# Four graph-attention layers on one core: a new order of work in the stages between the heads

## The chip, the cores and the metric

The kernel runs on one NeuronCore of a Trainium2 chip. The metric is the time of one execution on the device in microseconds (us), the median of several runs. Five engines work side by side, each through its own instruction list in order: TensorE (PE in the rows), VectorE (DVE), ScalarE (ACT), GpSimd (POOL) and SyncE (SP, which here only issues transfers). They wait for each other through semaphores that are written out by hand.

## The reference

`x` is (8 graphs, 1024 nodes, 128 features) and `adj` one 1024 x 1024 matrix for all graphs. Four layers follow each other, each closed by a residual and a norm:

```python
x = _layernorm(x + _L0_gnn_ref(x, adj, ...))   # 4 heads; inside: layernorm(attention @ Wo + bo + x) * gamma + beta
x = _layernorm(x + _L1_gnn_ref(x, adj, ...))   # 4 heads; inside: attention @ wo + bo
x = _layernorm(x + _L2_gnn_ref(x, adj, ...))   # 1 head of 128; leaky-relu scores; inside: elu(attention)
x = _layernorm(x + _L3_gnn_ref(x, adj, ...))   # 4 heads of 32; leaky-relu scores; inside: elu(attention)
```

Layer 0 thus has two norms after its attention (an inner one with gamma and beta, an outer one), the others have one.

## The kernel before

The kernel alternates between `node(stage)`, stages 0 to 4, and `heads(layer)`, layers 0 to 3. `heads` holds the attention and is not touched. `node(s)` closes layer s-1 (residual, norm) and opens layer s: it makes queries, keys and values (or, in stages 2 and 3, rows and columns of scores) of the new x and stores them to device memory. Stage 0 has nothing to close, stage 4 nothing to open.

A stage is a loop of rounds `i` from `-SKEW[stage]` to 7, written out in full on every engine. In round i each engine does the *closing* work of graph `f = i + SKEW[stage]` and the *opening* work of graph `i`. Before, SKEW is 2 in stage 1 and 1 in stages 2 to 4. So stage 1 has ten rounds, stages 2 to 4 nine, and in a round without a graph f (or a graph i) that half is left out.

Closing graph f, stages 1 and 2: PE transposes the attention's result (`turn_context`, L911) into PSUM banks 0 and 1; ACT copies it (`context`, L740); PE multiplies it (`contract`, L946, counted as y_ps) into banks 2 and 3; DVE adds x (`add_x`, L1262, event y) and takes mean and variance (`statistics`, L1249, event var); POOL raises them to the power -1/2 (`power`, event rstd); ACT applies that, eight instructions for the eight blocks of a graph (`norm`, L723; event xn). In stage 1 the first such norm is `inner_norm` (event z), then DVE does `scaled` (times gamma, plus `xplus`, which POOL made of x and beta in `plus_beta`, event xb), a second `statistics`, and ACT does `outer_norm`. In stages 3 and 4 the attention's result needs the ELU instead of a multiplication: ACT makes exp and relu of it (`below_zero`, L747, into the buffer `neg`), and DVE adds.

Opening graph i: PE transposes xn (`turn_x`, L917) into banks 4 and 5; ACT copies it (`turned`); PE multiplies queries and keys (`queries_keys`) or score rows (`rows_of`), then values into banks 0 and 1 (`by_blocks(0, ...)`), in stages 2 and 3 also columns (`columns_of`). ACT copies the first two (`high_parts`), then rounds the values to bf16 (`first_part`); DVE takes what is left (`project`: cv L1298, and the low parts of queries and keys), ACT rounds that (`second_part`), POOL what remains then (`last_part`, L650). SP stores all of it.

Since context and values share banks 0 and 1, `turn_context` waits until ACT and DVE have read the values (`values_read`).

The order inside a round of stage 1 before:

```
ACT:  context(f) turned(i) high_parts(i) first_part(i) inner_norm(f) second_part(i) outer_norm(i+1)
DVE:  add_x(f) statistics(f) project(i) scaled(i+1) statistics(i+1)
POOL: plus_beta(f) power0(f) last_part(i) power(i+1)
PE:   turn_context(f) turn_x(i) contract(f) queries_keys(i) values(i)
SP:   store_x(i) load(f+2) store_parts(i)
```

The loads of graph f+2 use the buffers of graph f, so SP waits for y, cT_ps and (stage 1) xb of f first (`used`).

## Time and profile before

| what | us |
|---|---|
| median of 3 runs (3216.36 to 3223.19) | 3221.73 |
| time of the profiled execution | 3225.56 |
| its span in the trace | 3223.8 |
| granted TensorE clock, mean | 0.83 of full speed |
| stage 1, first load issued to last copy of values by ACT | 749.3 to 1003.9 |
| stage 2, the same | 1755.9 to 1915.6 |
| stage 3, the same | 2258.6 to 2398.3 |
| stage 4, first load to last norm | 3109.1 to 3220.1 |

The table is read as a map: all that the diff touches lies in these four stretches (and in stage 0, up to about 125 us). The profiled execution has 1.8 us outside its span. A busy share over the whole span says little about a stage; what ends the waits in one round of each stage says more. A row of the windows view holds, from the left: the stretch, its length, the busy us (and instructions) of PE, PEld, DVE, ACT and POOL, the granted PE clock (1.00 is 2.4 GHz, 0.50 is 1.2 GHz), the busy share of the DMA engines and GB/s.

### The profile page before, as it was taken

The numbers are of one execution on the slowest core, as the hardware profiler recorded it, in microseconds if no ns is written. First come the engines' busy times: TensorE is split into PE (matmuls) and PEld (weight loads), VectorE is DVE, ScalarE is ACT, GpSimd is POOL, SyncE is SP. The second block draws the span as 40 slices with busy tenths as digits, with TensorE's granted clock in tenths as the row PEclk, the third lists the DMA queues.
The fourth block names the chain that finished last, engine by engine and source line by source line (L and its number), as shares of the span: only waits on it lengthen the run. The fifth ranks groups of instructions, "written<-read, shape, count | busy, mean of one in ns | idle before, by whom it ended". The sixth has DMA issues, their size and how long they took to land.

```text
span 3223.8 us, 90525 instructions
## 1 busy us (share of the span) xinstructions
PE 2378.1 (74%) x32777; PEld 1657.8 (51%) x33112; DVE 2195.8 (68%) x4654; ACT 1588.1 (49%) x2273; POOL 1827.9 (57%) x1837
## 2 busy tenths in 40 slices
PE   5588888884434988888886766888457999999950
PEld 3366666664332555555554544667234666666630
DVE  4499999994443777777776335452558988888943
ACT  3354444452441444444443543444555777777763
POOL 2388888885330665555566333444225777777851
PEclk9788888886665999999998667999667988888975
DMA  7822322223433112121212641110541111111134
GB/s 249 273 71 76 83 73 71 71 57 71 159 137 120 53 48 55 44 55 44 55 45 72 162 157 58 53 31 15 164 122 38 48 47 48 47 39 48 48 65 98
DMA packets 299864, 263.65 MB, mean 82 GB/s; under 512 B 193080, under 2 KB 257080, under 8 KB 299504
## 3 DMA queue, kind: packets, MB, share of 16 engines
q1 hardware_dynamic: 294896, 241.82, 27.3%
q0 software_dynamic: 4608, 16.78, 1.4%
q8 instruction: 257, 4.21, 0.5%
q14 instruction: 103, 0.84, 0.1%
HBM read 162.84 MB, written 95.36 MB: 80 GB/s over the span
## 4 chain that ended last, share of the span: by engine, by line
PE 29%; issue 15%; DVE 14%; ACT 4%; POOL 2%; DMA 2%; SPq 1%; DVEq 1%; POOLq 0%; ACTq 0%
PE ps L1107 11%; PE ps L1066 5%; DVE full L1393 4%; DVE full L1383 2%; PE ps L1004 2%; ACT xn L723 2%; POOL xc L333 2%; PE ps L1018 2%; PE ps L966 1%; PE ps L1064 1%; PE ps L1059 1%; DVE xn L1480 1%; DVE rden L1477 1%; PE ps L928 1%; PE ps L1051 1%
## 5 line engine op out<-in xcount | busy, mean ns | idle before, releaser
L333 POOL TENSOR_TENSOR xc<-part 128x512 f16<-128x512 f32 x1536 | 1579.2, 1054 | 805.1 <-ACT part L858 650.5
L1107 PE MATMUL ps<-vs,part 128*128 128x33 bf16 (+1 forms) x13824 | 847.6, 188 | 46.6 <-DVEq L1484 44.5
L1107 PEld LDWEIGHTS ps<-vs,part 128*128 128x128 bf16 x13824 | 676.2, 101 | 357.8 <-issue 198.0
L1107 PE MATMUL ps<-vs,xc 128*128 128x33 bf16 (+1 forms) x9216 | 777.0, 186 | 5.6 <-issue 5.6
L1107 PEld LDWEIGHTS ps<-vs,xc 128*128 128x128 f16 x9216 | 594.8, 99 | 0.0
L858 ACT ACTIVATE part<-ps 128x512 f32<-128x512 f32 x512 | 305.8, 597 | 432.6 <-PE ps L1051 432.4
L1393 DVE CUSTOM_DVE_ANT_0 full<-ps,mask_n 128x512 bf16<-128x512 f32 x512 | 353.0, 690 | 161.8 <-DVE top L1393 64.0
L1383 DVE CUSTOM_DVE_ANT_0 full<-ps,mask_n 128x1024 bf16<-128x1024 f32 x320 | 390.3, 1220 | 99.2 <-PE ps L1004 70.7
L840 ACT ACTIVATE part<-cv,lift 128x1024 f32<-128x1024 f32 x256 | 294.7, 1151 | 324.7 <-DVE cv L1414 298.1
L1066 PE MATMUL ps<-qs,sel 128*128 128x512 f32 x640 | 418.1, 655 | 14.3 <-ACT ps L832 14.2
L1047 PE MATMUL ps<-qs,ks 128*128 128x512 f32 x512 | 289.3, 568 | 120.8 <-DVE cv L1414 93.4
L1426 DVE SCALAR_TENSOR_TENSOR cv<-ks,colx,ps 128x512 f32<-128x512 f32 x320 | 238.7, 746 | 174.6 <-PE ps L1066 135.1
L858 ACT ACTIVATE part<-cv,cols 128x512 f32<-128x512 f32 x320 | 229.8, 718 | 239.0 <-DVE cv L1426 229.1
L1414 DVE SCALAR_TENSOR_TENSOR cv<-ps,mask_t 128x1024 f32<-128x1024 f32 x256 | 311.8, 1219 | 46.8 <-PE ps L1047 23.9
L1018 PE MATMUL ps<-ks,qs 96*128 96x512 f32 x512 | 253.1, 505 | 117.2 <-DVE top L1393 94.9
L1051 PE MATMUL ps<-qs,ks 97*128 97x512 f32 x512 | 307.7, 601 | 0.5
L858 ACT ACTIVATE part<-ps,colx 128x512 f32<-128x512 f32 x320 | 215.1, 672 | 74.2 <-PE ps L1066 69.2
L1089 PE MATMUL ps<-vs,part 128*128 128x99 bf16 x2048 | 233.0, 213 | 1.8 <-POOL xc L333 1.8
L1089 PEld LDWEIGHTS ps<-vs,part 128*128 128x128 bf16 x2048 | 164.5, 99 | 129.6 <-issue 106.3
L832 ACT ACTIVATE ps<-ks,colx 128x512 f32<-128x512 f32 x316 | 218.7, 692 | 11.5
L1091 PE MATMUL ps<-vs,xc 128*128 128x66 bf16 x2048 | 219.5, 195 | 0.0
L928 PE MATMUL ps<-ident,xn 128*128 128x128 f32 x256 | 56.5, 393 | 204.9 <-ACT xn L723 200.9
(151 smaller groups left out, 3591.8 us busy)
## 6 DMA issues: line engine op xcount, KB each, us to landing
qs<-q_d SPq DMA_DIRECT2D x224, 128.0 KB
ks<-k_d SPq DMA_DIRECT2D x224, 128.0 KB
ks<-row_d SPq DMA_DIRECT2D x40, 512.0 KB
vs<-v_d SPq DMA_DIRECT2D x96, 198.0 KB
q_d<-part SPq DMA_DIRECT2D x32, 512.0 KB
k_d<-part SPq DMA_DIRECT2D x32, 512.0 KB
ctx_d<-xn SPq DMA_DIRECT2D x96, 128.0 KB, 1.7
xc<-ctx_d SPq DMA_DIRECT2D x96, 128.0 KB, 4.3
```

The lines of the kernel that those rows point to most:

```text
L333: eng.tensor_tensor(plo[:, r, :], prob[:, r, :], phi[:, r, :], ALU.subtract).then_inc(low_done(layer, u, s)[0], 1)
L840: act.activation(prob[:, r:r + 2, :], arg[:, a:a + 2, :], ACT.Exp, scale=2.0 * CLIP, bias=lift[:, 0:1]).then_inc(s_exp, 2)
L858: act.activation(prob[:, r, :], src, ACT.Exp, **more).then_inc(s_exp, 1)
L1018: pe.matmul(bank, qs[0:96, n, it * P:(it + 1) * P], ks[0:96, n, cut], start=True, stop=True).then_inc(s_nsc, 1)
L1047: mm = pe.matmul(bank, ks[:, n, blk_j], qs[:, n, cut], start=True, stop=True)
L1051: mm = pe.matmul(bank, ks[0:97, n, blk_j], qs[0:97, n, cut], start=False, stop=True)
L1066: mm = pe.matmul(bank, sel[:, 2, :], qs[:, n, cut], start=False, stop=True, skip_group_check=True)
L1089: pe.matmul(ps[:, 6 + c, at_a:at_a + V3], phi[:, r, it * P:(it + 1) * P], vs[:, n, at_v:at_v + V3], start=opens, stop=False, skip_group_ch ...
L1107: mm = pe.matmul(acc, half[:, r, it * P:(it + 1) * P], vs[:, n, at:at + width], start=opens and h == 0 and v == 0, stop=h == 1 and v == 1, ...
L1383: dve.tensor_tensor_reduce(junk[:, :], pf[:, 4 * HALF:6 * HALF], mask_n[:, k, :], 1.0, LOWEST, ALU.add, ALU.max, accum_out=top[:, k, 0:1]) ...
L1393: dve.tensor_tensor_reduce(junk[:, 0:HALF], ps[:, 4 + c, :], mask_n[:, it, c * HALF:(c + 1) * HALF], 1.0, LOWEST, ALU.add, ALU.max, accum_ ...
L1414: dve.scalar_tensor_tensor(arg[:, a:a + 2, :], ps[:, r:r + 2, :], -0.5, mask_t[:, j:j + 2, c * HALF:(c + 1) * HALF], ALU.max, ALU.min).the ...
```

## The change

Eight edits, all in `node`:

1. SKEW of stages 2 and 3 goes from 1 to 2, so that these stages have ten rounds and graph i's xn is made two rounds before it is transposed.
2. `contract` writes y into banks 0 and 1, over the transposed context; `turn_context` of the next graph now waits for y of the graph before (DVE's `add_x`), not for the values.
3. The values get banks 2 and 3 for themselves (in stage 0 the keys move to banks 0 and 1).
4. In stage 1 DVE begins the round with `scaled(i+1)` and its statistics, and does `add_x(f)` and `project(i)` after them.
5. In stage 1 ACT does `outer_norm(i+1)` after `first_part(i)`, then `second_part(i)`, and `inner_norm(f)` last.
6. In stage 1 POOL begins with `power(i+1)`; `plus_beta(f)` goes to the end of its round.
7. In stage 1 SP loads graph f+2 after it has stored the parts of graph i.
8. In stages 3 and 4 `below_zero` runs one graph ahead: `below_zero(f+1)` stands in front of `outer_norm(f)`, `neg` has two buffers, and the wait for y is one graph looser.

```diff
-SKEW = (0, 2, 1, 1, 1)
+SKEW = (0, 2, 2, 2, 1)
...
-        xT, neg = cv[:, 2, :], cv[:, 3, :].rearrange("p (t f) -> p t f", f=F)
+        xT = cv[:, 2, :]
+        neg = [cv[:, k, :].rearrange("p (t f) -> p t f", f=F) for k in (0, 3)]
...
-            at = (6, 4)[w] if stage else (6, 2)[w]
+            at = (6, 4)[w] if stage else (6, 0)[w]
...
                     if stage and i >= 0:
                         store_x(i)
-                    if f + 2 < GRAPHS:
+                    if stage != 1 and f + 2 < GRAPHS:
                         used(f)
                         load_graph(stage, f + 2)
                     if stage < 4 and i >= 0:
                         store_parts(i)
+                    if stage == 1 and f + 2 < GRAPHS:
+                        used(f)
+                        load_graph(stage, f + 2)
...
+                    if stage == 1 and 0 <= i + 1 < GRAPHS:
+                        power(stage, "", i + 1)
                     if stage == 1 and f < GRAPHS:
-                        plus_beta(f)
                         power(stage, "0", f)
                     if stage > 1 and f < GRAPHS:
                         power(stage, "", f)
                     if stage < 4 and i >= 0:
                         last_part(i)
-                    if stage == 1 and 0 <= i + 1 < GRAPHS:
-                        power(stage, "", i + 1)
+                    if stage == 1 and f < GRAPHS:
+                        plus_beta(f)
...
-                    act.wait_ge(s_ev["y"], before("y", stage, b))
-                    act.activation(neg[:, :, :], cs[:, b % 2, :, :], ACT.Exp).then_inc(s_ev["ex"], 1)
+                    act.wait_ge(s_ev["y"], before("y", stage, b) - 1)
+                    act.activation(neg[b % 2], cs[:, b % 2, :, :], ACT.Exp).then_inc(s_ev["ex"], 1)
...
-                    if stage > 2 and f < GRAPHS:
-                        below_zero(f)
+                    if stage > 2 and f == 0:
+                        below_zero(0)
                     if stage < 4 and i >= 0:
                         turned(i)
                         high_parts(i)
                         first_part(i)
+                    if stage > 2 and f + 1 < GRAPHS:
+                        below_zero(f + 1)
+                    if stage == 1 and 0 <= i + 1 < GRAPHS:
+                        outer_norm(i + 1)
+                    if stage < 4 and i >= 0:
+                        second_part(i)
                     if stage == 1 and f < GRAPHS:
                         inner_norm(f)
-                    if stage < 4 and i >= 0:
-                        second_part(i)
-                    if stage == 1 and 0 <= i + 1 < GRAPHS:
-                        outer_norm(i + 1)
...
                 def turn_context(b):
                     pe.wait_ge(s_load[b % 2], load_at(stage, b // 2))
-                    values_read(max(a, 0))
+                    pe.wait_ge(s_ev["y"], before("y", stage, b))
...
-                    pe.wait_ge(s_ev["y"], before("y", stage, b))
-                    by_blocks(2, cT, wts[:, 4 * (stage - 1) + 3, :], 2 * stage - 1, "y_ps")
+                    by_blocks(0, cT, wts[:, 4 * (stage - 1) + 3, :], 2 * stage - 1, "y_ps")
...
-                        by_blocks(0, xT, wts[:, 4 * stage + 2 if stage < 2 else 6 + stage, :],
+                        by_blocks(2, xT, wts[:, 4 * stage + 2 if stage < 2 else 6 + stage, :],
...
+                    if stage == 1 and 0 <= i + 1 < GRAPHS:
+                        scaled(i + 1)
+                        statistics(i + 1, 1, "")
                     if stage and f < GRAPHS:
                         add_x(f)
                         statistics(f, 0 if stage == 1 else 1, "0" if stage == 1 else "")
                     if stage < 4 and i >= 0:
                         project(i)
-                    if stage == 1 and 0 <= i + 1 < GRAPHS:
-                        scaled(i + 1)
-                        statistics(i + 1, 1, "")
```

## Rows read from the trace of the kernel before

**Rows 1.** The page, part 1: busy time and share of the span.
```profile
PE 2378.1 (74%) x32777; PEld 1657.8 (51%) x33112; DVE 2195.8 (68%) x4654; ACT 1588.1 (49%) x2273; POOL 1827.9 (57%) x1837
```

**Rows 2.** Windows: one round of stages 1, 2, 3 and 4, in this order.
```profile
852.17:880.41 28.24, 12.08 (x60) 9.33 (x60) 13.51 (x38) 12.42 (x23) 9.67 (x10) 0.68 0.49 159
1803.08:1820.29 17.21, 13.44 (x70) 11.01 (x70) 7.14 (x22) 9.80 (x17) 8.10 (x12) 0.70 0.70 201
2294.80:2310.85 16.05, 9.70 (x44) 6.07 (x44) 10.09 (x26) 10.94 (x17) 4.44 (x5) 0.71 0.61 166
3142.13:3155.11 12.98, 0.00 (x0) 0.00 (x0) 4.74 (x18) 5.27 (x11) 2.35 (x4) 0.50 0.53 121
```

**Rows 3.** Timeline of ACT, stage 1: start, duration, line, out<-in, idle before and releaser.
```profile
760.35 1.02 ACT L743 ACTIVATE cv<-ps 128x1024 f32<-128x1024 f32 x1 [20.66 <-PE ps L914]
...
859.49 1.11 ACT L767 ACTIVATE part<-ps,bcol 128x1024 fp32r<-128x1024 f32 x1 [4.14 <-PE ps L957]
...
863.37 1.05 ACT L782 ACTIVATE vbuf<-ps 128x1024 bf16<-128x1024 f32 x1 [1.11 <-PE ps L941]
...
877.32 3.18 ACT L723 ACTIVATE xn<-full,rstd 128x128 f32<-128x128 f32 x8 [8.87 <-POOL rstd L634]
...
989.76 3.18 ACT L723 ACTIVATE xn<-full,rstd 128x128 f32<-128x128 f32 x8 [9.57 <-POOL rstd L634]
...
1003.94 1.05 ACT L782 ACTIVATE vs<-ps 128x1024 bf16<-128x1024 f32 x1 [1.11 <-PE ps L941]
```

**Rows 4.** Timeline of DVE, stage 1.
```profile
766.01 1.22 DVE L1268 TENSOR_TENSOR full<-ps,xc 128x1024 f32<-128x1024 f32 x1 [14.53 <-PE ps L941]
...
781.05 1.23 DVE L1268 TENSOR_TENSOR full<-ps,xc 128x1024 f32<-128x1024 f32 x1 [11.46 <-PE ps L941]
...
857.81 1.23 DVE L1268 TENSOR_TENSOR full<-ps,xc 128x1024 f32<-128x1024 f32 x1 [11.44 <-PE ps L941]
...
869.28 2.97 DVE L1279 TENSOR_TENSOR full<-full,vs 128x1024 f32<-128x1024 f32 x1
872.29 1.64 DVE L1252 BATCH_NORM_STATS2 bns<-full 128x6 f32<-128x128 f32 x8
873.97 0.64 DVE L1257 BATCH_NORM_AGGREGATE mv<-bns 128x2 f32<-128x6 f32 x8
```

**Rows 5.** Timeline of ACT, stage 2.
```profile
1811.16 1.01 ACT L773 ACTIVATE part<-ps 2x1024 f32<-2x1024 f32 x1 [4.91 <-PE ps L966]
...
1915.63 1.03 ACT L782 ACTIVATE vs<-ps 128x1024 bf16<-128x1024 f32 x1
```

**Rows 6.** Timeline of DVE, stage 2.
```profile
1792.19 1.23 DVE L1268 TENSOR_TENSOR full<-ps,xc 128x1024 f32<-128x1024 f32 x1 [12.25 <-PE ps L941]
...
1809.40 1.22 DVE L1268 TENSOR_TENSOR full<-ps,xc 128x1024 f32<-128x1024 f32 x1 [7.99 <-PE ps L941]
```

**Rows 7.** Timeline of ACT, stage 3.
```profile
2278.74 1.02 ACT L759 ACTIVATE cv<-ps 128x1024 f32<-128x1024 f32 x1
...
2299.55 1.01 ACT L773 ACTIVATE part<-ps 8x1024 f32<-8x1024 f32 x1 [3.73 <-PE ps L966]
...
2304.65 1.08 ACT L787 ACTIVATE vs<-cv 128x1024 bf16<-128x1024 f32 x1 [1.35 <-DVE cv L1298]
...
2398.28 1.02 ACT L782 ACTIVATE vs<-ps 128x1024 bf16<-128x1024 f32 x1
```

**Rows 8.** Timeline of ACT, stage 4.
```profile
3126.04 3.18 ACT L723 ACTIVATE xn<-full,rstd 128x128 f32<-128x128 f32 x8 [7.85 <-POOL rstd L634]
...
3142.13 1.04 ACT L749 ACTIVATE cv<-xc 128x1024 f32<-128x1024 f32 x1
...
3216.95 3.18 ACT L723 ACTIVATE xn<-full,rstd 128x128 f32<-128x128 f32 x8 [7.68 <-POOL rstd L634]
```

**Rows 9.** Timeline of SP's queue, stage 4: the four context loads of one graph.
```profile
3134.37 3.69 SPq L416 DMA_DIRECT2D xc<-ctx_d  x4
```

**Rows 10.** DMA issues of stage 4: count, KB each, median us to landing.
```profile
xc<-ctx_d SPq DMA_DIRECT2D x32, 128.0 KB, 4.2
```

## What the change will do, and by how much

> **What bounds the kernel now.** I began with the page's busy shares [rows 1]: no engine is above 74% of the span, so waits set the pace somewhere. All that the diff touches lies in the stages between the heads, so I laid a window over one round of each stage [rows 2]. There no engine is near full: of a round of 28.24 us in stage 1 ACT works 12.42, DVE 13.51, PE 12.08; in stage 2 (17.21 us) PE 13.44 and ACT 9.80; in stage 3 (16.05 us) ACT 10.94; in stage 4 (12.98 us) ACT 5.27 and nobody more. A round is a loop of waits. The timelines give the loop, and the reader is to look at the brackets. In stage 1 ACT waits 8.87 us for POOL's rstd before the outer norm [rows 3]: DVE first takes apart the values of graph i, and only then scales graph i+1. The next round's context copy stands behind that norm, and y behind the copy. In stage 2 the two waits are those for PE, 4.91 us among them [rows 5]. In stage 3 ACT waits 3.73 us for the rows and 1.35 us for DVE, the rest is its own work: 10.94 + 3.73 + 1.35 = 16.0, the round [rows 2, 7]. In stage 4 ACT waits 7.68 us for rstd of the graph whose ELU it has just made [rows 8].
>
> **Stage 1.** What is removed is the wait of the outer norm for DVE's second half. I lay out a new round on ACT, from the start of context(f) at 0.
> - Context to y: at 760.35 ACT starts the copy with nothing else on PE, at 766.01 DVE starts on y: 5.66 us [rows 3, 4]. That is at the lower clock.
> - y to the queries' copy: 859.49 - 857.81 = 1.68. To the values' copy: 863.37 - 859.49 = 3.88 [rows 3, 4]. So values at 11.2.
> - Values 0.95; then outer_norm(i+1), 3.1 (a row's 3.18 less the overlap with the next); second_part 1.0; inner_norm(f) 3.1. Next context at 19.4. The same by counting: 12.42 of work and some 7 of waits for PE that remain.
>
> Is each input there? scaled(i+1) needs z from the end of the round before: DVE starts at 0.1 and takes 1.25 + 1.25 + 2.32 for scaling, addition and statistics [rows 4]. The addition at L1279 took 2.97 where it met POOL's last_part, against 1.23 for such a size alone [rows 4]; now scaling meets plus_beta instead. I allow 1.7 more: var(i+1) at 6.6. From the end of the aggregation at 874.61 to the norm at 877.32 are 2.71 [rows 3, 4]: rstd at 9.3, needed at 12.2. y at 5.66 waits up to 1 us for DVE, then var0(f) by 10.2 and rstd0 by 12.9, needed at 16.3. The values' remainder on DVE ends at 12.2 + 3.6 = 15.9 (1.23 for vf and the two low parts), when PE may turn the next x, as the next round needs at 19.4. All of it is covered; if the cover of rstd (2.9 us) were gone, each us would lengthen the round by one.
>
> The moved load: plus_beta(f) is now last on POOL, after last_part, which follows second_part at 16.3; POOL's whole work is 9.67 us a round [rows 2], so these two end by about 21.5. Only then does SP issue load(f+2), behind four stores of queries and keys, one of values, one x. Issue takes 4.1 (0.4 + 3.69), the last context load lands 4.2 after its issue [rows 9, 10]; in all some 9 us with the stores in front, at 30.5, or 11 into the next round. turn_context(f+2) comes up on PE after that round's values, at 11.2, and turn_x behind it is held until 15.9 anyway; 4 us are to spare.
>
> Clock: PE's work of a round now lies in shorter stretches with shorter pauses. The y term above is priced at the lower level; I add 0.5 for queries that still begin low. Round: 19.9.
>
> Ends: y(1) stays at 781.05. statistics 3.58, rstd 2.71, inner norm 3.1: round 0 starts at 790.4. Six rounds of 19.9: 909.8. Round 6 has no context: the values' copy comes 11.0 after the end of the outer norm before it (989.76 + 3.18 to 1003.94 [rows 3]), of which 2.1 are transposes already made: 8.9; outer_norm(7) then ends at 909.8 + 8.9 + 0.95 + 3.2 = 922.9; 0.6 until DVE frees the keys' bank; 11.0: last values at 934.5. Before 1003.94. **Gain 69.4.** Bounds: the ACT sum with no clock term (19.4) 72, a round of 22.5 53.
>
> **Stage 2.** One round more, xn(i) early, banks apart. From the context copy 0: y at 5.66 instead of 6.32 (1803.08 [rows 2] to 1809.40 [rows 6]), since PE no longer turns x first; the rest of the round, 10.89, stays: 16.55. PE then works 13.4 of 16.5 and may find the higher clock a bit earlier: 16.4. Ends: y(1), without turn_x before it but behind outer_norm(0), is 0.9 earlier, 1791.3; 3.6 + 2.7 + 3.1 to the start of round 0, 1800.6; six rounds, 98.4, to 1899.0; round 6 without a graph f takes 13.1 (values' copy 7.5 after that of x, DVE up to the columns 3.5, turning 2.1); then 7.5: 1919.6. Before 1915.63 [rows 5]. **Loss 4.0**: the freed wait is worth less than the added round. Bounds: y at 3.5 after the copy, with PE at the higher clock (the 4.58 us from the start of `contract` to y halved to about 2.4), makes the round 14.4 and a gain of 8; rows too at the lower clock (18.1), a loss of 14.
>
> **Stage 3.** The ELU of f+1 stands where ACT waited 1.35 for DVE, so that wait is covered; the 3.73 for the rows stay, as x is now turned early but the copy and the product still follow each other: 14.7. Round 0's x copy moves behind outer_norm(1): from 2278.74 to 2282.4. Then 7 x 14.7 + 7.5: 2392.8, before 2398.28 [rows 7]. **Gain 5.5.** Bounds: 0 (SP's store of x now has to be done within the same round, it is issued some 10 us ahead of the norm) and 17 (rows at the higher clock, 13.0).
>
> **Stage 4.** The loop ELU, add, statistics, power, norm is opened. ACT works 5.27 [rows 2]; power(f) must wait for xn(f-1), since rstd has one buffer, so norm to norm is at least 2.7 + 3.1 = 5.9. But the loads follow: SP issues load(f+2) only behind the store of xn(f-1). From xn(f-1): store 0.4, x 0.4, three context issues 2.8, 4.2 to landing [rows 9, 10], and about 1.2 because the stored 512 KB now lie directly in front: 9.0. Then ELU 2.15 and norm 3.2 give xn(f+1): 14.4 for two graphs, 7.4 a graph with the gaps between instructions. The DMA engines agree: 0.53 x 12.98 = 6.9 us of work per graph [rows 2]. Norms from 3126.04: two distances of 5.9 and five of 7.4, last one at 3174.8 instead of 3216.95 [rows 8]. **Gain 42.** Bounds: 45 if the store costs nothing in front; 27 with 9.5 us a graph.
> The Trainium skill ("DMA: Bandwidth & Descriptors", section "Why small descriptors are slow") counts a fixed overhead of about 3 bus cycles per packet, which for the 128-byte pieces of the context loads leaves 4 of 7. By its 435 GB/s a graph's 512 KB would take an estimated 2.1 us. The window's 6.9 us leave about 4.4 for them after two large transfers of 1.25, so the trace shows them slower than the page has it; by the page the sum would be some 5 us lower.
>
> **Stage 0** keeps its waits, the banks only change names: 0. The heads: 0.
>
> **Sum.** 69.4 - 4.0 + 5.5 + 42.1 = 113. The profiled execution of 3225.56 (span 3223.8) would become 3112.6; the median of the runs is 3.8 lower, so 3221.7 - 113 = 3109.
>
> **Rivals.**
> 1. *PE holds the higher clock in the closer rounds.* For it: the pauses shrink, in stage 2 to 3 us of 16. Against: in stage 2 PE is busy 13.44 of 17.21 even now and has 0.70 [rows 2]. Stage 1 rounds of 17.3 (16 more), stage 2 a gain of 8 instead of a loss of 4, stage 3 a gain of 17: 3109 - 16 - 12 - 12 = 3069.
> The Trainium skill ("TensorE: Matmul & The Clock Gate", section "HAM oscillation — how this bites in real kernels") says that pauses make the clock fall and each burst begin cold, and that work without long pauses keeps it up. It speaks for this rival; row 0.70 at 78% busy speaks for less.
> 2. *The loads bind.* DMA work is 0.49 x 28.24 = 13.8 us a round in stage 1, 12.0 in stage 2 [rows 2]; if the bursts collide, stage 1 goes to 24 and stage 4 to 9.5: 25 + 15 less gain, 3149.
> 3. *DVE and POOL collide more than allowed*, as POOL's two additions are now adjacent and DVE starts just there: rstd late by 3 us a round in stage 1, 22.9, 18 less gain: 3127.
> 4. *Slower.* The load of stage 1, put behind xb and the stores, misses its graph and PE waits for it in order. It has 4 us to spare; to eat 113 us over six rounds it must be 4 + 19 = 23 us late. At 25 late: 6 x 2 over the even point, 3234.
> 5. *The change doesn't do what it says in stage 1*: DVE still finds z or xb late, the round stays at 28.2; 3178. The z norm ends the ACT round, which speaks against it.
>
> **Chances.** As worked out 0.54 (its own range 3092 to 3127); rival 1 0.12, rival 2 0.15, rival 3 0.11, rival 4 0.04, rival 5 0.04. What is left out of 3076 to 3150 is rivals 1, 4 and 5, 0.20. 0.2% (6 us) is about what a measurement of this kernel tells from no change. Faster 0.94, same 0.02 and slower 0.04.
>
> **What the profile after would show.** Right: y-to-y distances of 20, 16.4, 14.7 us in stages 1 to 3; the outer norm of stage 1 with no wait for POOL; ten rounds in stages 2 and 3; norm-to-norm 5.9 once and then 7.4 in stage 4, with ACT's exp waiting for the DMA. Wrong: an rstd wait of some us in stage 1 (rival 3), `turn_context` waiting for a DMA there (2, 4), PE clock above 0.8 in the stages (1).

## The result and the profile after

The changed kernel takes 3119.5 us (median; 3117.63 to 3143.97) against 3220.43 of before: 0.9701 of its time, 95% interval 0.9658 to 0.9744. Run again, beside experiments 1 to 3, it took 3123.56, ratio 0.9702 (0.9673 to 0.9731); one of the 17 executions of the kernel before that were timed with these, 4280.64 us at a granted clock of 1.00, is not counted. Predicted were 3109, in a range of 3076 to 3150. The execution whose trace is read here is a long one, 3143.97 (span 3142.2); the third row below shows why, a stretch in which the change alters nothing.

Windows of the profile after, from SP's first load for a stage to the first load of the heads behind it: stage 1, stage 2, heads 2, stage 3, stage 4. The columns are those of [rows 2]: length, busy time of PE, its weight loads, DVE, ACT, POOL, granted clock, DMA share, GB/s.
```profile
750.60:947.38 196.78, 112.72 (x480) 82.61 (x480) 104.33 (x305) 98.24 (x176) 75.17 (x82) 0.70 0.59 183
1688.71:1864.93 176.22, 109.30 (x560) 83.54 (x560) 57.12 (x176) 78.17 (x120) 64.76 (x90) 0.66 0.55 157
1864.93:2217.65 352.72, 278.76 (x2850) 213.65 (x2850) 151.49 (x328) 133.87 (x192) 135.81 (x145) 0.81 0.14 44
2217.65:2366.25 148.60, 82.28 (x368) 50.36 (x368) 85.28 (x209) 87.43 (x128) 40.69 (x42) 0.67 0.52 143
3065.16:3142.20 77.04, 0.00 (x0) 0.00 (x0) 37.89 (x144) 42.78 (x80) 22.37 (x32) 0.50 0.73 164
```
The same stretches cut from the kernel before, and from the changed kernel run again:

| us | before | after | after, again | predicted change |
|---|---|---|---|---|
| up to the first heads | 129.8 | 133.7 | 133.1 | 0 |
| heads 0 | 619.5 | 616.9 | 615.0 | 0 |
| stage 1 | 267.1 | 196.8 | 196.5 | -69.4 |
| heads 1 | 739.5 | 741.3 | 742.6 | 0 |
| stage 2 | 169.9 | 176.2 | 178.4 | +4.0 |
| heads 2 | 332.8 | 352.7 | 332.8 | 0 |
| stage 3 | 152.7 | 148.6 | 148.4 | -5.5 |
| heads 3 | 697.7 | 698.9 | 698.7 | 0 |
| stage 4 | 114.8 | 77.0 | 76.7 | -42.1 |

Heads 2 has the same instructions in all three (2850 weight loads). In the twelve other profiles of this study, the kernel before among them, it takes 331.5 to 334.7 us at a granted clock of 0.85 or 0.86; this one shows 352.7 at 0.81. The second profile has the normal value, and there the sum is -101.6 of the predicted -113.

What the reader can see of the single steps. Stage 1, ACT's timeline, profile after:
```profile
857.98 1.11 ACT L772 ACTIVATE part<-ps,bcol 128x1024 fp32r<-128x1024 f32 x1 [6.41 <-PE ps L963]
...
861.86 1.05 ACT L787 ACTIVATE vs<-ps 128x1024 bf16<-128x1024 f32 x1 [1.11 <-PE ps L948]
862.80 3.16 ACT L728 ACTIVATE xn<-full,rstd 128x128 f32<-128x128 f32 x8
865.87 1.07 ACT L792 ACTIVATE vs<-cv 128x1024 bf16<-128x1024 f32 x1
866.84 3.17 ACT L728 ACTIVATE full<-full,rstd 128x128 f32<-128x128 f32 x8
869.91 1.00 ACT L748 ACTIVATE cv<-ps 128x1024 f32<-128x1024 f32 x1
...
934.99 1.05 ACT L787 ACTIVATE vs<-ps 128x1024 bf16<-128x1024 f32 x1 [1.11 <-PE ps L948]
```
The outer norm at 862.80 has no bracket where it had 8.87 us of wait for POOL [rows 3]. From the values' copy (861.86) to the next context copy (869.91) ACT works without a gap. What remains are its waits for PE. The distance between the starts of `add_x` of two graphs, y to y, is the length of a round: 18.7 to 20.2 us in the full rounds. The last values come at 934.99; 934.5 was forecast.

Stage 2, PE's timeline, the same profile:
```profile
1776.93 1.07 PE L921 MATMUL ps<-ident,xc 128*128 128x128 f32 x8
1779.90 1.94 PE L935 MATMUL ps<-ident,xn 128*128 128x128 f32 x8 [1.90 <-DVE colp L1325]
1783.68 0.61 PE L940 MATMUL ps<-bias,ones_b 65*128 65x512 bf16 x1 [1.84 <-ACT cv L748]
1784.08 1.92 PE L948 MATMUL ps<-wts,cv 128*128 128x128 f32 x8
...
1788.06 2.27 PE L972 MATMUL ps<-cv,aa 128*2 128x512 f32 x4
```
There are two pauses of under 2 us a round. From the first of them on PE runs at the 1.2 GHz level: eight transposes take 1.94 us where those in front of the pause took 1.07. The clock comes back within the rows' product (L972), so that 10.2 us of this round are at the low level and the rest at 2.4 GHz (granted clock 0.70). Stage 2's round is 16.5 to 17.0 us instead of the forecast 16.4.

Stage 4, ACT's timeline, the same profile:
```profile
3083.97 3.19 ACT L728 ACTIVATE xn<-full,rstd 128x128 f32<-128x128 f32 x8 [4.91 <-POOL rstd L638]
...
3096.05 1.06 ACT L754 ACTIVATE cv<-xc 128x1024 f32<-128x1024 f32 x1 [2.14 <-DMA xc<-ctx_d]
...
3102.83 1.06 ACT L754 ACTIVATE cv<-xc 128x1024 f32<-128x1024 f32 x1 [1.46 <-DMA xc<-ctx_d]
...
3106.52 3.18 ACT L728 ACTIVATE xn<-full,rstd 128x128 f32<-128x128 f32 x8 [1.46 <-POOL rstd L638]
...
3118.81 1.06 ACT L754 ACTIVATE cv<-xc 128x1024 f32<-128x1024 f32 x1 [2.89 <-DMA xc<-ctx_d]
...
3135.29 3.18 ACT L728 ACTIVATE xn<-full,rstd 128x128 f32<-128x128 f32 x8 [3.04 <-POOL rstd L638]
```
The wait of 7.68 us for rstd [rows 8] is down to 1.46 or nothing between the first norm and the last, and the exps wait for their context loads, as forecast. Seven norm-to-norm distances add to 3135.29 - 3083.97 = 51.3 us, 7.3 each; the sum had 48.8.

### The profile page after: what moved, and what is told of

Read it like the earlier page. It is cut to its first block, busy times and chain, and to the rows that moved or that the text cites. A ratio compares the mean times of both kernels' runs of the same rounds, so it can differ in the third digit from the quotient of the medians.

```text
span 3142.2 us, 90847 instructions
## 1 busy us (share of the span) xinstructions
PE 2413.1 (77%) x33112; PEld 1668.6 (53%) x33112; DVE 2194.8 (70%) x4654; ACT 1585.7 (50%) x2273; POOL 1829.2 (58%) x1837
## 4 chain that ended last, share of the span: by engine, by line
PE 38%; issue 22%; DVE 22%; ACT 7%; POOL 3%; DMA 2%; DVEq 1%; SPq 1%; ACTq 0%; POOLq 0%
PE ps L1113 13%; PE ps L1072 4%; DVE xn L1458 4%; DVE full L1399 4%; PE ps L1010 3%; DVE full L1389 2%; PE ps L948 2%; PE ps L1053 2%; ACT xn L728 2%; PE ps L1065 2%; DVE cv L1420 2%; PE ps L1070 2%; POOL xc L334 2%; PE ps L1024 2%; PE ps L972 2%
## 5 line engine op out<-in xcount | busy, mean ns | idle before, releaser
L1095 PEld LDWEIGHTS ps<-vs,part 128*128 128x128 bf16 x2048 | 164.2, 99 | 129.8 <-issue 103.9
L1056 PE MATMUL ps<-mask_t,ident_b 128*128 128x512 bf16 x512 | 205.0, 400 | 0.4
```

Of the source, the lines that this page charges most:

```text
L1095: pe.matmul(ps[:, 6 + c, at_a:at_a + V3], phi[:, r, it * P:(it + 1) * P], vs[:, n, at_v:at_v + V3], start=opens, stop=False, skip_group_ch ...
```

## The experiments

Lengths of stages are cut from the traces as above. The changed kernel's are 196.5, 178.4, 148.4 and 76.7 us (after, again); stages that an edit doesn't touch came out within 2.5 us of that. An edit's effect on a stage is read from one profile each, so a difference of 2 to 3 us says nothing. The rest scatters more: the time up to the first heads lay anywhere from 129.3 to 133.7, heads 0 from 613.8 to 619.5, and heads 3 from 693.7 to 712.5.

**1. The kernel again, and the skew of stage 2 back at 1.**

> The changed kernel unchanged, profiled and timed again. In its first profile (3142.2 us) the attention of layer 2, which the diff does not touch, took 352.7 us from its first unit load to the next stage's first load, against 332.8 before, at a granted clock of 0.83 against 0.90; three other executions of the same kernel were 22 to 26 us shorter. Theory: TensorE falls into one of two rhythms there, by chance of phase, and in a profile near 3117 us this stretch is back near 333 us with a clock near 0.90, while the stages between the heads keep their lengths of 196.8, 176.2, 148.6 and 77.0 us within 2 us. Rival: the change itself lengthens it (other bank use, other landing times); then it is 352 us again and the 25 us are lost elsewhere. Ratio to before 0.968.

The theory held: 3123.56 us, heads 2 back at 332.8 us, the stages 196.5, 178.4, 148.4 and 76.7. (The expectation's clocks, 0.83 and 0.90, leave out the two ends of heads 2; over the whole of it they are 0.81 and 0.86.) What made it slow once is open. Two of the executions of the kernel before timed here also lie over 20 us above its median (3241.46 and 3243.39, clock 0.828 against 0.835), without a trace that shows where.

> The changed kernel with SKEW of stage 2 back at 1, all else kept. My theory (the freed wait is worth less than the added round): stage 2 goes from 176.2 us back to about 170 (round near 17.2 us, nine rounds), so this kernel is 6 us faster than the changed one. Rival (the skew pays, the 6 us come from the shared banks): the length stays at 176 or grows to 190, because y and the context now share banks 0 and 1 and turn_context waits for y.


```diff
-SKEW = (0, 2, 2, 2, 1)
+SKEW = (0, 2, 1, 2, 1)
```
3115.04 us, ratio 0.9677 (0.9644 to 0.9710); stage 2 takes 168.9 us, with y-to-y distances of 17.0 to 17.1 against 16.5 to 17.0. So the second graph ahead shortens hardly any round in stage 2, and the round more costs 7.3 or 9.5 us, by the first or the second profile of the changed kernel. The clock is part of that: the stage's granted clock is 0.71 here and 0.66 or 0.65 there. With fillers on PE (experiments 6 and 9) the same two skews give 165.9 and 152.5 us, 13.4 apart. The 169.9 of before the change lie within the scatter of 168.9, so the separate banks by themselves do nothing here that can be told.

**2. The ELUs in turn.**

> The changed kernel with the ELU of a graph made in its own round again (two buffers and the looser wait kept). My theory: stage 4 goes from 77 us back to 115 (round 13.0 us), stage 3 from 148.6 to 158 (its round from 14.5 to 15.8, since the 1.35 us wait for DVE is open again); together 45 us slower than the changed kernel, ratio to before 0.983. Rival: the two buffers and the looser wait alone already give part of it, stage 4 at 90 to 100 us.


```diff
-                    if stage > 2 and f == 0:
-                        below_zero(0)
+                    if stage > 2 and f < GRAPHS:
+                        below_zero(f)
...
-                    if stage > 2 and f + 1 < GRAPHS:
-                        below_zero(f + 1)
```
3172.93 us, ratio 0.9846 (0.9811 to 0.9882). Stage 3 161.8, stage 4 115.3 us. ACT in its stage 4:
```profile
3098.45 3.18 ACT L728 ACTIVATE xn<-full,rstd 128x128 f32<-128x128 f32 x8 [7.67 <-POOL rstd L638]
3101.54 1.04 ACT L754 ACTIVATE cv<-xc 128x1024 f32<-128x1024 f32 x1
```
The loop of before is back with its wait of 7.67 and its round of 12.98 [rows 2, 8]; the buffers and the looser wait alone give nothing. The early ELU is worth all of stage 4's gain, and 13.4 us in stage 3: with the skew of 2 but ELUs in turn that stage is 9 us longer than before the change.

**3. DVE's and POOL's old order in stage 1**, all else changed.

> The changed kernel with DVE's and POOL's old place for the second norm of stage 1 (after the values' remainder), ACT's new order kept. My theory: this one edit carries stage 1. The outer norm waits again for DVE: values 12.2, remainder 3.6, scaling and statistics 4.8, power 2.7, norm 3.1, second part 1.0, inner norm 3.1: a round of 30 us, slower than before the change (28.2); stage 1 about 265 us instead of 196.8, ratio to before near 0.99. Rival: the freed banks and the later inner norm carry it; then the round stays at 20 to 23 us.


```diff
                 for i in range(-SKEW[stage], GRAPHS):
                     f = i + SKEW[stage]
-                    if stage == 1 and 0 <= i + 1 < GRAPHS:
-                        scaled(i + 1)
-                        statistics(i + 1, 1, "")
                     if stage and f < GRAPHS:
                         add_x(f)
...
                         project(i)
+                    if stage == 1 and 0 <= i + 1 < GRAPHS:
+                        scaled(i + 1)
+                        statistics(i + 1, 1, "")
```
(and POOL's `power` of i+1 behind that of f.) 3204.47 us, ratio 0.9949 (0.9922 to 0.9977). Stage 1 takes 281.1 us in rounds of 30.7, 14 more than before the change; the theory had 265 and rounds of 30. ACT's timeline there:
```profile
872.96 1.05 ACT L787 ACTIVATE vbuf<-ps 128x1024 bf16<-128x1024 f32 x1 [1.11 <-PE ps L948]
885.16 3.18 ACT L728 ACTIVATE xn<-full,rstd 128x128 f32<-128x128 f32 x8 [11.15 <-POOL rstd L638]
```
The wait is back at 11.15, more than the 8.87 of before. By the orders, that is because ACT now has the late norm ahead of two operations that were ready, 4.0 us of work.

**4. ACT's old order in stage 1**, with DVE's and POOL's new one.

> The changed kernel with ScalarE's order of before in stage 1 (first norm, second part of V, second norm), and DVE's and POOL's new order. Theory A, formed on the run in which DVE and POOL alone had their old order (round 30.7 us, longer than the 28.2 of before): the two orders belong together, since a round of the new kernel is set by xn, TensorE and the evictions of q, k and V, after which ScalarE starts the second norm without a wait for POOL. With the old order the first norm (3.17) and the second part (about 1) come in between, so xn is ready some 4 us later: round about 23.5 instead of 19.7, stage 1 about 197 + 7 x 3.8 = 224 us, the whole about 3150. Theory B: only DVE's order mattered, ScalarE's could have stayed: round 19.7 to 20.5, stage 1 up to 203, the whole at 3122 to 3130.


```diff
-                    if stage == 1 and 0 <= i + 1 < GRAPHS:
-                        outer_norm(i + 1)
-                    if stage < 4 and i >= 0:
-                        second_part(i)
                     if stage == 1 and f < GRAPHS:
                         inner_norm(f)
+                    if stage < 4 and i >= 0:
+                        second_part(i)
+                    if stage == 1 and 0 <= i + 1 < GRAPHS:
+                        outer_norm(i + 1)
```
One run, 3128.2 us; stage 1 201.4 us, y-to-y 18.3 to 20.1. Theory A fell, B holds: DVE's order is what counts. The full rounds are 19.7 us on average, as in the changed kernel; most of the 5 us lies in one distance at the start of the stage (18.3 against 14.5). ACT's timeline of it:
```profile
863.97 3.18 ACT L728 ACTIVATE full<-full,rstd 128x128 f32<-128x128 f32 x8 [0.38 <-POOL rstd L638]
867.06 1.06 ACT L792 ACTIVATE vs<-cv 128x1024 bf16<-128x1024 f32 x1
868.03 3.17 ACT L728 ACTIVATE xn<-full,rstd 128x128 f32<-128x128 f32 x8
871.10 1.00 ACT L748 ACTIVATE cv<-ps 128x1024 f32<-128x1024 f32 x1
```
Both norms still stand between the values' copy and the context copy, only swapped, so the next round begins at the same place; my theory had counted xn's delay and forgotten that the context copy, not xn, heads the round.

**5. The skew of stage 3 back at 1**, ELUs still ahead.

> The changed kernel with a skew of 1 instead of 2 in stage 3, as before the change; the ELUs are still begun a graph ahead and V keeps its own banks. Theory A (the second graph ahead is what takes POOL's rstd and the norm off the chain that sets stage 3's round): round 15.5 to 16, as in the kernel before (16.05), less one round at the start: stage 3 148.4 + 8 x 1.3 - 9 = about 150, the whole within 3 us of the changed kernel. Theory B (the skew carries the gain in full): round 16.7, stage 3 about 158, the whole +10. Theory C (the ELU begun ahead and V's banks alone do it, as stage 2 showed for its skew): round 14.5, stage 3 about 140, the whole -8.


```diff
-SKEW = (0, 2, 2, 2, 1)
+SKEW = (0, 2, 2, 1, 1)
```
3128.31 us, ratio 0.9714 (0.9674 to 0.9755); stage 3 160.2 us, rounds of 16.7 to 17.0. Its timeline of PE:
```profile
2282.38 1.97 PE L935 MATMUL ps<-ident,xn 128*128 128x128 f32 x8 [5.60 <-ACT xn L728]
2285.46 3.58 PE L972 MATMUL ps<-cv,aa 128*8 128x512 f32 x4 [1.11 <-ACT cv L764]
```
PE waits for a norm that stands behind the ELU on ACT. Theory B: in stage 3 either half of the change alone makes it longer (160.2 and 161.8 against 152.7 before); the two together make 148.4. Both halves have the banks apart; no run shows what the banks do in this stage by themselves.

**6. PE's pauses in stage 2 filled.**

> The changed kernel with 16 further matmuls of the bias row (65x512, results not used) in each full round of stage 2: 8 between the turned context and the turned x, 8 between the turned x and the context's contraction, where TensorE pauses for 1.90 and 1.84 us. Theory A: these two pauses are what keeps the granted clock at the low level in the half of the round behind them (turned x 1.94 us, contraction 1.92 a half, rows 2.36, where the other half shows 1.07, 1.05); filled, the clock stays high, each filler of 8 takes about 1.8 us and so fits its pause, and a round goes from 17.0 to about 14 us (TensorE's work at high clock 9 to 10 us, with the waits for ScalarE behind it): stage 2 178.4 - 6 x 3 = about 160, the whole about 3105. Theory B: the clock stays low in that half, the fillers take about 3.4 us each in place of a pause of 1.9, and each round is 1.5 to 3 us longer: stage 2 187 to 196, the whole about 3135.


```diff
+                def filler(bank):
+                    for _ in range(8):
+                        with_bias(bank, 0)
...
+                    if has_f and has_a and stage == 2:
+                        filler(5)
                     if has_a:
                         turn_x(i)
+                    if has_f and has_a and stage == 2:
+                        filler(2)
```
3116.19 us, ratio 0.9674 (0.9634 to 0.9714). Stage 2 falls to 165.9 us, rounds of 14.47; theory A had 160 and the whole at 3105. Most of the gain is lost again in heads 3, which takes 707.3 us in this profile instead of 698.7, for a reason that is open. PE's timeline:
```profile
1784.38 1.07 PE L921 MATMUL ps<-ident,xc 128*128 128x128 f32 x8
1785.29 1.89 PE L940 MATMUL ps<-bias,ones_b 65*128 65x512 bf16 x8
1787.35 1.06 PE L935 MATMUL ps<-ident,xn 128*128 128x128 f32 x8 [0.17 <-DVE colp L1333]
1788.25 1.89 PE L940 MATMUL ps<-bias,ones_b 65*128 65x512 bf16 x8
1791.13 0.39 PE L940 MATMUL ps<-bias,ones_b 65*128 65x512 bf16 x1 [0.99 <-ACT cv L748]
1791.36 1.05 PE L948 MATMUL ps<-wts,cv 128*128 128x128 f32 x8
```
x8 in 1.05 where it was 1.92: the 2.4 GHz level holds through the whole round, and each filler fits its pause. The work left to do is the same, so the 12.5 us (10 to 14 against the 176.0 to 179.5 of all profiles that have this stage unchanged) are the price of the clock in this stage. The Trainium skill ("TensorE: Matmul & The Clock Gate", section "A second HAM failure mode: psum-queue depth-cycling") tells of a kernel in which small idles between groups of matmuls, not long waits, made the clock go up and down; the trace agrees, with pauses of 1.90 and 1.84 us.

**7. Stage 4: the loads ahead of the store.**

> The changed kernel, but in stage 4 SP issues the loads of graph f+2 before the store of graph i, so that they wait for y (which frees the buffers) and no longer for xn. In the changed kernel y's second operation ends 0.5 us before xn in one round and 2.1 us before it in another, and the store's issue takes 0.4 us. Theory A (the loads' start sets ScalarE's wait for them): loads start 0.9 to 2.4 us earlier a round, a round of 7.2 falls to 6.0 to 6.5, stage 4 from 76.7 to 69 to 72 us. Theory B (what sets it is the issue of the four context loads, 4.8 us, and the transfers behind them, with the 16 DMA engines 74% busy over the stage): the loads land hardly earlier and stage 4 stays at 75 to 77 us. The whole moves by 7 us at most.


```diff
-                    if stage and i >= 0:
+                    if stage and stage < 4 and i >= 0:
                         store_x(i)
...
                         load_graph(stage, f + 2)
+                    if stage == 4 and i >= 0:
+                        store_x(i)
```
3116.7 us, ratio 0.9687 (0.9635 to 0.9738), not to be told from the changed kernel as a whole; stage 4 72.9 us, between the theories and nearer to A, rounds of 6.76, one of 7.14. ACT's timeline:
```profile
3072.13 1.04 ACT L756 ACTIVATE cv<-xc 128x1024 f32<-128x1024 f32 x1
3073.21 1.15 ACT L758 ACTIVATE cv<-cv,unit 128x1024 f32<-128x1024 f32 x1
3075.81 3.18 ACT L730 ACTIVATE xn<-full,rstd 128x128 f32<-128x128 f32 x8 [1.45 <-POOL rstd L640]
3078.90 1.04 ACT L756 ACTIVATE cv<-xc 128x1024 f32<-128x1024 f32 x1
```
No exp waits for a load any more, though the DMA engines are 79% busy over the stage.

**8. Stage 4: long pieces.**

> The changed kernel, with the four context loads of a graph in stage 4 each as 1 KB pieces into two whole rows of blocks, in place of 128-byte pieces scattered over all rows: the same bytes, but the context's columns then stand in another order than the reference's, so its output is another. It takes the cost of the short pieces away and leaves the order of all engines. Theory A (the short pieces set ScalarE's wait for the context loads, 1.1 to 3.0 us in most rounds of stage 4): the issue of the four loads falls from 4.8 to 1.5 to 2 us, the exps never wait for DMA, the round is then that of the norms (ScalarE 5.4 us busy, or 1.45 us of wait for POOL's rstd as well) at 5.5 to 6.7 us in place of 7.2, stage 4 is 64 to 71 us instead of 76.7. Theory B (bytes or the start of the loads set it): 74 to 77.


```diff
                     for k in range(4):
+                        if stage == 4:
+                            sp.dma_start(cs[:, q, 2 * k:2 * k + 2, :],
+                                         one(ctx_d, b * 4 + k).rearrange("a p t f -> (a p) (t f)")
+                                         ).then_inc(s_load[q], 16)
+                            continue
```
This kernel leaves out the reference's order of the context's columns, as the expectation says. One run, 3113.6 us; stage 4 72.0 us, again between the theories. SP's timeline of it, and under it that of the changed kernel at the same point:
```profile
3067.07 0.39 SPq L430 DMA_DIRECT2D out<-xn  x1
3067.51 0.58 SPq L411 DMA_DIRECT2D xc<-x_d  x1
3068.13 2.59 SPq L418 DMA_DIRECT2D xc<-ctx_d  x4
```
```profile
3093.94 0.40 SPq L425 DMA_DIRECT2D out<-xn  x1
3094.38 0.58 SPq L411 DMA_DIRECT2D xc<-x_d  x1
3095.00 5.08 SPq L417 DMA_DIRECT2D xc<-ctx_d  x4
```
With the same bytes the issue of the four loads takes 2.59 us instead of 5.08 and the DMA share falls from 0.73 to 0.55. But an earlier start (7) gives the same stage to within 1 us: beyond 4 to 5 us neither helps. A loop over two graphs is then left. In the trace of experiment 7 it is norm 3.1, ELU 2.2, y to the end of the aggregation 5.0 and power 3.2, each with the gap behind it: 13.5 us, which is two rounds of 6.76.

**9. Fillers in stages 1 to 3**, with the skew of 1 in stage 2 from experiment 1 and the loads of experiment 7.

> Four edits to the changed kernel, each in a stage of its own, so that each is read from its stage's length. Stage 1: 16 filler matmuls of the bias row before the turned context, 12 behind the turned x (where TensorE pauses 4.1 and 2.8 us a round). Stage 2: a skew of 1, and 20 fillers before the turned x (the pause there is 4.8 us with a skew of 1, and 8 + 8 fillers held the clock at 2.4 GHz with a skew of 2). Stage 3: 16 fillers before the turned x, 5 behind it (pauses 3.7 to 4.1 and 1.2). Stage 4: the loads of graph f+2 ahead of the store. Theory A (the pauses hold the clock low in all three stages, and TensorE at the low level is on the chain that sets each round): stage 1: the contraction 3.9 to 2.0 us, round 19.7 to about 17.7, length 196.5 to about 181; stage 2: round 14.5 with one round fewer than with a skew of 2, 165.9 to about 155; stage 3: turned x 1.94 to 1.07 and rows 3.58 to 1.9, round 14.5 to 12.0, length 148.4 to about 128; stage 4 72.9 again. The whole about 3060. Theory B (only stage 2 was so near the bound that filling helped): stages 1 and 3 at their lengths or up to 3 us a round longer by the fillers at low clock, the whole 3100 to 3120. If heads run slower behind fuller stages, their lengths show it: 741, 332.8 and 698.6 in the changed kernel.


```diff
+                    if stage == 1 and b >= SKEW[1]:
+                        filler(0, 16)
                     for it in range(BLOCKS):
                         mm = pe.transpose(pf[:, it * P:(it + 1) * P], cs[:, b % 2, it, :], ident[:, :])
...
+                    if has_f and has_a and stage == 2:
+                        filler(5, 20)
+                    if stage == 3 and i > 0:
+                        filler(0, 16)
                     if has_a:
                         turn_x(i)
+                    if has_f and has_a and stage == 1:
+                        filler(2, 12)
...
+                    if stage == 3:
+                        filler(0, 5)
```
3093.37 us, ratio 0.9618 (0.9594 to 0.9642). Stage 1 190.4, stage 2 152.5, stage 3 140.3, stage 4 72.5: 6, 26, 8 and 4 us less than in the changed kernel. The gains of stages 1 and 3 are smaller than theory A's (lengths of 181, 155 and 128 in the first three stages, 3060 in all) and larger than theory B's; heads 3 took 712.5 in this profile. In stage 1 the rounds were 17.8 and 19.8 in turn, and PE's timeline showed why:
```profile
851.77 5.58 PE L948 MATMUL ps<-bias,ones_b 65*128 65x512 bf16 x16 [1.26 <-DMA xc<-ctx_d]
857.14 1.91 PE L929 MATMUL ps<-ident,xc 128*128 128x128 f32 x8
...
870.80 3.62 PE L948 MATMUL ps<-bias,ones_b 65*128 65x512 bf16 x16
874.26 1.04 PE L929 MATMUL ps<-ident,xc 128*128 128x128 f32 x8
```
A filler behind a wait does not fill it. In every other round the 16 stood behind the load's wait of 1.2 to 1.3 us; the clock fell after the first seven of them, and the other nine and the transposes behind them ran at the low level.

**10. The fillers ahead of the load's wait.**

> The kernel of all four edits once more, with what its trace showed mended. Stage 1: the 16 fillers now stand ahead of the wait for the context load (they stood behind it, and in every other round TensorE waited 1.26 us for that load, the fillers then ran at the low level, 5.6 us in place of 3.6, and the round was 19.8 in place of 17.8), and 14 in place of 12 behind the turned x. Stage 3: 18 and 9 fillers in place of 16 and 5, which leaves less of the pauses of 0.7 and 1.0 us. Stage 2: 21 in place of 20. Theory A (every pause above about 1 us is a chance for the clock to fall, and filling it removes the low rounds): stage 1 all rounds at 17.8, length 190.4 to about 182; stage 3 all rounds at 12.85 (6 were, 2 were 15.9 and 14.5), length 140.3 to about 134; the whole 3093 to about 3079. Theory B (the clock falls at some rounds however full TensorE is, and more fillers then only delay the turned x further): stage 3 140 to 146, stage 1 186 to 192, the whole 3090 to 3105.

Against experiment 9, the numbers of fillers apart:
```diff
-                    pe.wait_ge(s_load[b % 2], load_at(stage, b // 2))
                     pe.wait_ge(s_ev["y"], before("y", stage, b))
                     if stage == 1 and b >= SKEW[1]:
                         filler(0, 16)
+                    pe.wait_ge(s_load[b % 2], load_at(stage, b // 2))
```
3080.11 us (3069.23 to 3100.53), ratio 0.9583 (0.9557 to 0.9610), the fastest here. Stage 1 takes 183.2 us in rounds of 17.2, at a granted clock of 0.82 where the changed kernel has 0.70: theory A holds there. The move is not alone in that, as the two fillers more behind the turned x share in it: the rounds of 17.8 became shorter too. Heads 3 is at 694.7. In stage 3, 142.4 us, theory B holds. PE there:
```profile
2218.38 6.15 PE L948 MATMUL ps<-bias,ones_b 65*128 65x512 bf16 x18
2224.33 1.91 PE L943 MATMUL ps<-ident,xn 128*128 128x128 f32 x8
...
2233.94 4.04 PE L948 MATMUL ps<-bias,ones_b 65*128 65x512 bf16 x18
2238.24 1.07 PE L943 MATMUL ps<-ident,xn 128*128 128x128 f32 x8 [0.25 <-DVE colp L1343]
```
There is no wait ahead of the first row, and none of more than 0.25 us on PE in the 20 us before it, and still the clock fell within it. The 18 fillers then take 2.1 us more than at 2.4 GHz and push the turned x back: a round of 15.6 instead of 12.85. Why it falls there is open.

## Why the prediction came out as it did

**Stage 1, right.** The wait removed was the one named, and 69.4 us of gain became 70.6 (267.1 to 196.5); the full rounds take 19.7 on average against 19.9. All covers held in the full rounds: no wait for rstd in the outer norm, no wait of `turn_context` for its load (PE's first wait in a round is for DVE's keys). The load's cover was there, but only as far as the forecast counted it, to `turn_x`: in the profile after, the last context load landed at 861.22, `turn_context` began at 861.66 and `turn_x` at 866.75. Experiment 3 shows that without DVE's and POOL's new order nothing of the gain is left, and experiment 4 that with it and ACT's old order 65.7 of the 70.6 us come. What the separate banks and the later load add in this stage, no run took apart; experiment 3, which has both, shows that they give nothing without DVE's order. The allowance of 1.7 us for DVE's collision with POOL's addition fits: scaling took 2.44 us at 870.03 where L1277 took 1.2 alone, 1.2 more.

**Stage 2, the sign right, the size not.** 4.0 us of loss were forecast, 6.3 and 8.5 came. The step that was off is "the rest of the round, 10.89, stays". The context copy to y took 5.64 us (5.66 forecast), but y to the next context copy rose from 10.9 in the first rounds to 11.4: the rows' product, 1.88 us before the change, takes up to 2.40 since it now begins at the low level (1.88 in the first two rounds of the first profile), and PE did not "find the higher clock a bit earlier" as I had it. Six full rounds of 16.9 instead of 16.4 are 3.2 of the 4.5 us that are missing in the second profile; the first has some rounds of 16.5 and lost 6.3. A slip beside it: from the start of `contract` to y the trace before has 4.41 us, not 4.58; only a bound rests on that. Experiment 1 then shows what the added round costs with next to nothing given back, 7.3 to 9.5 us.

**Stage 3, right in size.** 5.5 us forecast, 4.1 and 4.3 measured; rounds of 14.5 to 14.9 against 14.7. What the prediction had not seen is that it takes both edits (experiments 2 and 5).

**Stage 4, mechanism right, size 4 us off.** 42.1 forecast, 37.7 and 38.1 measured. Two steps: the first norm comes 1.8 us late, and the term for the norms from then on was 48.8 and measured 51.3. None of the distances was 5.9, at which two were priced; the shortest are 6.22, 6.23 and 6.76. The term also let the norm follow the ELU at once, but in three rounds ACT waited 1.45 us for rstd behind the ELU, because `power` was not done by then. The first power took longer beside DVE, in POOL's timeline of the profile after:
```profile
3079.53 1.12 POOL L633 TENSOR_SCALAR rstd<-mv 128x8 f32<-128x8 f32 x1 [18.10 <-DVE mv L1263]
3080.71 1.19 POOL L634 TENSOR_SCALAR rstd<-mv 128x8 f32<-128x8 f32 x1
...
3089.68 1.01 POOL L638 TENSOR_TENSOR rstd<-rstd 128x8 f32<-128x8 f32 x1
```
Each of the first two takes 0.24 in other rounds; here DVE's two operations of y, from 3079.32 to 3081.79, lie beside them. The last one takes 0.2 elsewhere; beside DVE's y of 3089.41 it takes 1.01 and makes the second `power` 3.4 us instead of 2.7, which is most of 6.76 against 5.9. That one caused the other is read from their places, no run separated them. That the loads set rounds was forecast, and experiment 7 shows it for the 4 us between 76.7 and 72.9.

**What was put at nothing.** The stretch up to the first heads was 3.3 us longer in the second profile, and the heads 0.4 shorter in sum. With stage 1 (-1.2), stage 2 (+4.5), stage 3 (+1.2) and stage 4 (+4.0) that is the whole difference between -113 and -101.6. The 3.3 lies within the 129.3 to 133.7 that the other kernels show there, which leave that stretch alone.

**The rivals.** Rival 1 (the clock rises by itself) did not come: 0.70, 0.66 and 0.67 in stages 1 to 3, after 0.65, 0.66 and 0.67. Its mechanism is real, though: given fillers, stage 1 becomes 13.3 us shorter (priced at 16), stage 2 12.5 with its skew left alone (12), stage 3 6 to 8 (12). Rival 2 holds a grain in stage 4 (4 us), none in stage 1. Rivals 3, 4 and 5 did not occur; experiment 3 shows what rival 5 would have been.

## What to carry to other kernels

When one engine waits for a norm, look for the engine two steps up that does something less urgent first, and change that order first: in stage 1 DVE's and POOL's alone gave 66 of the 71 us, ACT's alone cost 14. Half a reordering can cost more than it gives (stage 3 with either half +7 to +9 us). A deeper skew costs a round more, and pays only where it shortens the others. In a loop that TensorE shares, filling its pauses can be worth more than moving waits: in stage 2 fillers gave 12.5 us where the deeper skew cost 7.3 to 9.5. The fillers have to stand ahead of a wait and end before it does, and a gain in one stage can go lost in the heads behind it (heads 3 in experiments 6 and 9).

## What the runs showed of the hardware

- In stage 2, with pauses of 1.84 and 1.90 us in a round of 17, 10.2 us of it ran at the 1.2 GHz level; with the pauses filled down to 0.17 and 0.99 the whole round ran at 2.4 GHz. In stage 3 of experiment 10 the clock fell in two rounds with no pause over 0.25 us in them.
- Heads 2 in one execution ran at a granted clock of 0.81 and took 18 to 21 us longer than in the twelve other profiles (0.85 to 0.86), with no instruction changed.
- The issue of four context loads took 3.5 to 5.5 us in stage 4 with pieces of 128 bytes, and 1.9 to 2.6 with pieces of 1 KB, for the same 512 KB.
- DVE's scaling in stage 1 (128x1024 f32, two inputs in SBUF) took 1.23 us at 791.53, after POOL's addition of the same size had ended, and 2.43 to 2.45 us in the six rounds in which it began beside that addition.
